# A routed two-layer kernel on one core: four input groups in flight, GpSimd's loop bounds read later, low halves ahead of VectorE's turn

## The chip, the cores and the metric

The kernel runs on 1 core of one Trainium2 chip. The metric is the device time of one execution in microseconds (us), lower is better. The kernel before was timed three times: 565.46, 571.8 and 562.29 us, median 565.46 us.

## The reference, cut to what matters

The input x is 128 graphs of 64 nodes with 128 features, 8192 tokens in all. First comes a graph attention layer over every graph, then a mixture of 8 experts of which each token takes 2:

```python
x = x + elu(softmax(where(adj > 0, leaky(e_src + e_dst), -inf)) @ (layernorm(x) @ W))   # one adjacency for all graphs
h = layernorm(x)
scores = h @ Wg.T + bg
top2, idx = top_k(scores, 2);  p = softmax(top2)
for e in range(8):                      # hidden width 512
    y = relu(h @ W1[e].T + b1[e]) @ W2[e].T + b2[e]
    out += combine[..., e] * y          # combine holds p at the two chosen experts
x = x + out
```

All data is float32.

## The kernel before, in words

The program is written engine by engine; the order on each engine is the order of the code, and engines wait for each other on semaphores only.

**Stage 1, 16 groups of 512 tokens.** Group g lies in `x_all[:, g]`. A step t works on five groups at five stages at once: normalisation and attention scores of group t, softmax and attention product of t-1, residual, second norm and gate of t-2, top-2 choice of t-3, and slot numbers of t-4. SyncE (SP) loads x in `_(sp)`: groups 0 and 1 at L399 and L405, then a loop (L408) of two bodies; body q waits for the last landing on `x_in[q]` and then issues the next group (L412), so two groups are in flight. Behind that loop stand in SP's queue the expert weights `w1_raw`, `w2_raw` (L415, L416) and biases, and then the copies of normalised rows into `rows` (L432, `pass_on`). VectorE waits for `x_in` ahead of its statistics (L812 and L1024). GpSimd waits for the last groups of x (L489, L490), then fills the sure blocks' slots with pads (L491), and from step 4 on sends each group's 1024 rows to their slots in HBM with 8 indirect DMAs (L504).

**Stage 2, expert blocks of 512 slots.** Block i is loaded into `xs`, transposed (PE L1401), rounded to a high part (ACT L681) and a low part (DVE L1107). TensorE does 12 matmuls for the hidden layer (L1417, L1418, L1421; four chunks, each with `w1_hi` on the high part, `w1_lo` on the high part, `w1_hi` on the low part), then transposes of the next block's x and of the last block's y (L1401, L1409), then 12 for the result (L1430, L1431, L1433). ScalarE (ACT) does the relus (L686, L690), the rounding of the next block and the result's bias (L696). VectorE's `turn(i, b, sent)` halves the four chunks of block i+1, makes the low part of block i+2, and weighs block i's result (`weigh`, L1122) with its row numbers (`ysi`, L1124). `ysi` releases GpSimd's `send_rows` (L521): 4 indirect DMAs per block into `moe_rows`. There are four buffers b; from block 4 on `weigh` first waits until the rows of block i-4 have landed (`scattered[b]`).

Blocks 0 to 7 (two of each of experts 0 to 3) are sure to exist; how many more each expert has is known only when all tokens are routed. `block_table()` writes `until_i` on VectorE. After its turns 1, 2 and 3 VectorE works out `pairs` and `rest`, the numbers of trips of the last loops of GpSimd and VectorE, and releases `pairs_ok`. GpSimd's `pairs_and_rest(pool)` waits for it and loads two registers from `until_i` (L368). `low_halves(e)` (L1100) makes `w1_lo` and `w2_lo` of expert e as raw minus high; it waits for ACT's `high_halves(e)` (L562, L564), and TensorE waits for it (`lo_ok`) ahead of block 2e.

The first blocks run beside the last steps of stage 1 (`drain()` on each engine). At the end SP reads the rows back (L466), TensorE, GpSimd (L529) and VectorE (L1276) add them to x, and ACT stores.

Of the kernel before, what the change touches and what calls it, by code (L numbers as in the profile page):

```python
# [21 lines left out]
GROUPS = TOKENS // GROUP  # L22
# [6 lines left out]
AHEAD = 4  # L29
# [14 lines left out]
STAGES = 5  # L44
MASKED = -1e30
META = 4
LEAD = 2
FIRST = 1
HIGH, LOW = 14, 15
# [26 lines left out]
def gnn_moe_kernel(nc, x, adj, w, wt, a, wg_t, bg, w1_t, b1_t, w2_t, b2_t, consts, out):  # L76
    ctx = ExitStack()
    with ctx:
# [3 lines left out]
        def sem(name):  # L82
            return ctx.enter_context(nc.semaphore(name))
# [40 lines left out]
        x_all = sb("x_all", [P, GROUPS, SUB, D])  # L124
# [206 lines left out]
        out_ok = sem("out_ok")  # L331
        due_met = sem("due_met")
        moe_got, moe_got1 = ([sem(f"{n}{g}") for g in range(GROUPS)] for n in ("moe_got", "moe_got1_"))
        x_in, rows_out = ([sem(f"{n}{q}") for q in range(2)] for n in ("x_in", "rows_out"))
        scattered = [sem(f"scattered{b}") for b in range(BUFS)]

        def tiles(ap):
# [27 lines left out]
        def pairs_and_rest(eng):  # L365

            eng.wait_ge(pairs_ok, 1)
            return [eng.value_load(until_i[0:1, E + n:E + n + 1], min_val=1, max_val=most) for n, most in ((0, 2 * E), (1, 2))]  # L368
# [26 lines left out]
        @block.sync  # L395
        def _(sp):
            sp.dma_start(a_sb[:, :], a).then_inc(c_a, 16)
            sp.dma_start(cst[:, :], consts).then_inc(c_cst, 16)
            sp.dma_start(x_all[:, 0, :, :], x_groups[0]).then_inc(x_in[0], 16)  # L399
            sp.dma_start(wt_sb[:, :], wt).then_inc(c_wt, 16)  # L400
            sp.wait_ge(int_zeros, 1)
            sp.dma_start(adj_i[0:NODES, 0:NODES], adj).then_inc(c_adj0, 16)
            sp.dma_start(adj_i[NODES:P, NODES:P], adj).then_inc(c_adj1, 16)
            sp.dma_start(w_sb[:, :], w).then_inc(c_w, 16)
            sp.dma_start(x_all[:, 1, :, :], x_groups[1]).then_inc(x_in[1], 16)  # L405
            sp.dma_start(wg_sb[:, :], wg_t).then_inc(c_wg, 16)
            sp.dma_start(bg_sb[:, :], bg.partition_broadcast(P)).then_inc(c_bg, 16)
            with sp.Fori(1, GROUPS // 2) as m:  # L408
                for q in range(2):

                    sp.wait_ge(x_in[q], 16 * m)
                    sp.dma_start(x_all[:, bass.ds(2 * m + q, 1), :, :],  # L412
                                 x_groups[bass.ds(2 * m + q, 1)].rearrange("g p s d -> p g s d")).then_inc(x_in[q], 16)

            sp.dma_start(w1_raw[:, :, :], w1_t).then_inc(c_w1, 16)  # L415
            sp.dma_start(w2_raw[:, :, :, :], w2_t).then_inc(c_w2, 16)  # L416
            sp.dma_start(b1_sb[:, :, :], b1_t).then_inc(c_b1, 16)
            sp.dma_start(b2_sb[:, :], b2_t).then_inc(c_b2, 16)

            def pass_on(m, q):  # L420

                g = 2 * m + q
                xn2_due, sent, passed = [v if isinstance(v, int) else nc.snap(v) for v in
                                         (SUB * g + SUB, 16 * 2 * SUB * m, 32 * g)]

                sp.wait_ge(xn2_ok, xn2_due)
                if later(m):
                    sp.wait_ge(rows_out[q], sent)
                if later(g):
                    sp.wait_ge(rowx_ok, passed)  # L430
                for k in range(2):
                    sp.dma_start(rows[q][:, k, :, 0:D], xn2[q][:, :, :]).then_inc(rowx_ok, 16)  # L432

            for q in range(2):
                pass_on(0, q)
            with sp.Fori(1, SURE_GROUPS // 2 + 1) as m:
                for q in range(2):
                    pass_on(m, q)
            pass_on(SURE_GROUPS // 2 + 1, 0)
            load_block(sp, sure_row(0), 0)  # L440
            pass_on(SURE_GROUPS // 2 + 1, 1)
            for q in range(2):
                pass_on(GROUPS // 2 - 1, q)

            sp.wait_ge(table_ok, 1)
            bounds = [SURE_BLOCKS]
            for q in range(2):
                sp.wait_ge(rows_out[q], 16 * 2 * SUB * (GROUPS // 2))
            n = sp.value_load(count_i[0:1, E - 1:E], min_val=0, max_val=TOKENS)
            for k in range(LEAD):  # L450
                sp.dma_start(slots[bass.ds(n + ((E - 1) * CAP + (k + 1) * GROUP), GROUP), :].rearrange("(p s) r -> p s r", s=SUB),
                             pad_rows[:, (E - 1) % 2, :, :]).then_inc(beyond_out, 16)
            for e in range(E - 1):
                bounds.append(block_bound(sp, e))
                sp.wait_ge(pads_out, 16 * max(e + 1, 2))
                with sp.Fori(bounds[e], bounds[e + 1]) as i:
                    row = nc.s_assert_within((i - bounds[e]) * GROUP + rest_row(e), rest_row(e), (e + 1) * CAP - GROUP,
                                             skip_runtime_bounds_check_because="an expert has at most TOKENS tokens")
                    load_block(sp, row, i)
            bounds.append(block_bound(sp, E - 1))  # L460
            sp.wait_ge(pads_out, 16 * E)
            for n in range(LEAD):
                load_block(sp, (E - 1) * CAP + n * GROUP, bounds[E - 1] + n)

            def read_plane(k, g):
                sp.dma_start(moe_in(k, g), moe_groups[k, g]).then_inc((moe_got, moe_got1)[k][g], 16)  # L466

            sp.wait_ge(late_ok, 4)
            for k in range(2):
                for h in range(GROUPS // 2):  # L470
                    due = bounds[E - 1 + k]
                    if h < GROUPS // 2 - 1:
                        due = sp.value_load(late_i[0:1, h:h + 1, k], min_val=1, max_val=MOST_BLOCKS)
                    sp.wait_ge(landed, due)
                    sp.sem_inc(due_met, 1)
                    for g in (2 * h, 2 * h + 1):
                        read_plane(k, g)

        @block.gpsimd
        def _(pool):  # L480
# [4 lines left out]
            nc.gpsimd.tensor_copy(pad_rows[:, 0, :, ID].bitcast(I32), cst[:, C_PAD:C_FULL]).then_inc(pads_ok, 1)  # L485
            nc.gpsimd.tensor_scalar(pad_rows[:, 1, :, ID].bitcast(I32), cst[:, C_PAD:C_FULL], float(GROUP), None, ALU.add).then_inc(pads_ok, 1)
            pool.wait_ge(pads_ok, 2)
            for q in range(2):
                pool.wait_ge(x_in[q], 16 * (GROUPS // 2))  # L489
            for i in range(SURE_BLOCKS):  # L490
                nc.gpsimd.dma_start(slots[sure_row(i):sure_row(i) + GROUP, :].rearrange("(p s) r -> p s r", s=SUB),  # L491
                                    pad_rows[:, i // 2 % 2, :, :]).then_inc(sure_out, 16)
# [14 lines left out]
                                in_=rows[q][:, k, j, :], in_offset=None).then_inc(rows_out[q], 16)  # L507

            by_steps(pool, step)
            pairs, rest = pairs_and_rest(pool)  # L510

            def send_rows(i, b, landings=()):

# [20 lines left out]
            for b in range(BUFS - 1):  # L534
                pool.wait_ge(scattered[b], QUADS * (16 * SUB))
            pool.sem_inc(landed, BUFS * QUADS - 1)
            with pool.Fori(0, pairs) as n:

                send_rows(2 * n + BUFS * QUADS, 0, ((3, QUADS), (1, n + QUADS)))
                send_rows(2 * n + (BUFS * QUADS + 1), 1, ((0, n + (QUADS + 1)),))  # L540
# [240 lines left out]
        def _(dve):  # L781
# [27 lines left out]
            def first_stats(b):  # L809

                for g in range(BATCHES[b].start, BATCHES[b].stop):
                    dve.wait_ge(x_in[g % 2], 16 * (g // 2 + 1))  # L812
                    for j in range(SUB):
                        last = nc.vector.bn_stats(bn1[:, g - BATCHES[b].start, j, :], x_all[:, g, j, :])
                last.then_inc(stats1_ok, 1)
                dve.wait_ge(stats1_ok, b + 1)
                for g in range(BATCHES[b].start, BATCHES[b].stop):
                    for j in range(SUB):
                        last = nc.vector.bn_aggr(mv1[:, g, j, :], bn1[:, g - BATCHES[b].start, j, :])
                last.then_inc(aggr1_ok, 1)  # L820
                dve.wait_ge(aggr1_ok, b + 1)
                nc.vector.tensor_scalar(var1[:, BATCHES[b], :], mv1[:, BATCHES[b], :, 1], EPS, None, ALU.add).then_inc(var1_ok, 1)
# [192 lines left out]
            def step(t, groups, q, m):  # L1015
# [5 lines left out]
                    add_bases(gr)  # L1021
                    write_slots(gr, q, m)
                if gx is not None and norms(gx) > 1:
                    dve.wait_ge(x_in[q], 16 * (m + 2))  # L1024
                    for j in range(SUB):
                        nc.vector.bn_stats(bn3[:, j, :], x_all[:, bass.ds(gx + AHEAD, 1), j, :].rearrange("p g d -> p (g d)"))
                if gx is not None:
# [113 lines left out]
            def turn(i, b, sent):  # L1141

                dve.wait_ge(ys_ok, i + 1 + FIRST)
                for c in range(HC):
                    halve(i + 1, c)
                low_x(i + 2)
                weigh(i, b, sent)
# [67 lines left out]
            by_steps(dve, step, GROUPS + 1)  # L1215
            drain()
            for b in range(1, BUFS):
                turn(b, b, 0)
                if b > 1:
                    low_halves(b)  # L1220
            nc.vector.tensor_scalar(until_i[:, E:E + 1], until_f[:, E - 1:E], 0.5, 0.75 - FULL, ALU.mult, ALU.add
                                    ).then_inc(blocks_ok, 1)
            dve.wait_ge(blocks_ok, 5)
# [311 lines left out]
```

## Time and profile before

| | us |
|---|---|
| three timed runs | 565.46, 571.8, 562.29 |
| median | 565.46 |
| span of the profiled execution | 568.7 |
| time of the profiled execution outside its span | not recorded |
| TensorE busy in the span | 455.3 (80%) |
| VectorE / ScalarE / GpSimd busy | 362.3 / 319.5 / 291.6 |

The span runs from the first to the last instruction of one execution. The profile was taken on one execution; a timed run may wait at other places. Start times below are counted from the span's start. In a timeline row the bracket tells how long the engine sat idle ahead of the instruction and who released it; "remote" is a releaser that the profile doesn't attribute, and "issue" is time in which the engine waited for nothing that the profile shows.

### The profile page before, as it was taken

To read this page: it belongs to the slowest core of one execution; us is meant where nothing else is said; L and a number is where in the kernel's file an instruction comes from. 1 tells how busy PE (TensorE), PEld (TensorE's weight loads), DVE (VectorE), ACT (ScalarE), POOL (GpSimd) and SP (SyncE) were. 2 spreads that over 40 slices of the span, in tenths; PEclk is the share of its full clock that TensorE was granted. 3 is DMA by queue.
4 is the path that set the end of the run, shared out by engine and by line. 5 is a ranking of instruction groups with operands and counts; after the bars stand their busy time and mean duration, and the time that the engine had idled before them with its cause. 6 is when DMAs were issued, how large, how long until landed. Compare 5 with 4: busy or idle time off the path is not lost.

```text
span 568.7 us, 9056 instructions
## 1 busy us (share of the span) xinstructions
PE 455.3 (80%) x2231; PEld 333.3 (59%) x2246; DVE 362.3 (64%) x1410; ACT 319.5 (56%) x760; POOL 291.6 (51%) x292
## 2 busy tenths in 40 slices
PE   8798377786666667868879866999999899989881
PEld 4566245564555445656658634777777687867530
DVE  6689257666556554667657625677767667756763
ACT  2778145655445455554558724667677577746600
POOL 1033755564444455445712775656765466565462
PEclk9999677878778888757989976999999999999986
DMA  5595322221122223223232312332332323256689
GB/s 137 169 378 175 93 75 72 71 80 58 42 66 70 76 76 93 65 81 94 66 108 66 85 51 73 95 99 74 93 95 72 95 74 93 79 168 203 184 270 318
DMA packets 56291, 63.03 MB, mean 111 GB/s; under 512 B 7744, under 2 KB 40896, under 8 KB 56000
## 3 DMA queue, kind: packets, MB, share of 16 engines
q1 hardware_dynamic: 35728, 33.28, 20.1%
q0 software_dynamic: 9344, 20.10, 10.5%
q10 hardware_dynamic: 11184, 9.26, 5.4%
q8 instruction: 12, 0.20, 0.1%
q14 instruction: 23, 0.19, 0.1%
HBM read 27.28 MB, written 26.94 MB: 95 GB/s over the span
## 4 chain that ended last, share of the span: by engine, by line
PE 49%; another core or an unknown queue 15%; ACT 12%; issue 9%; DVE 8%; DMA 3%; POOL 2%; SPq 1%; ACTq 0%; POOLq 0%; DVEq 0%
PE bank L1417 5%; PE bank L1421 5%; PE bank L1433 5%; PE bank L1418 4%; PE bank L1430 4%; PE bank L1431 4%; PE bank L1377 4%; PE bank L1318 4%; PE bank L1379 3%; ACT prob L591 3%; PE bank L1299 3%; PE bank L1409 2%; PE bank L1401 2%; ACT hh L690 2%
## 5 line engine op out<-in xcount | busy, mean ns | idle before, releaser
L504 POOL DMA_INDIRECT expert_slots<-rows,slot_i x128 | 127.6, 997 | 122.3 <-DVE slot_i L868 85.6
L1430 PE MATMUL bank<-hh,w_hi 128*128 128x512 f32 x144 | 63.4, 441 | 12.7 <-issue 4.5
L1417 PE MATMUL bank<-xh,w_hi 128*128 128x512 f32 x144 | 62.5, 434 | 7.3 <-ACT xh L681 4.8
L1318 PE MATMUL bank<-wh,prob_t 128*128 128x128 f32 x128 | 27.6, 383 | 48.4 <-ACT prob_t L599 39.0
L521 POOL DMA_INDIRECT moe_rows<-hrelu,ysi x40 | 41.9, 1048 | 43.1 <-issue 37.7
L696 ACT ACTIVATE yb<-bank,b_sb 128x512 f32<-128x512 f32 x36 | 24.8, 690 | 68.9 <-PE bank L1433 42.6
L1433 PE MATMUL bank<-hl,w_hi 128*128 128x512 f32 x144 | 60.6, 421 | 0.0
L1418 PE MATMUL bank<-xh,w_lo 128*128 128x512 f32 x144 | 59.5, 413 | 0.0
L1421 PE MATMUL bank<-xl,w_hi 128*128 128x512 f32 x144 | 59.2, 411 | 0.0
L1431 PE MATMUL bank<-hh,w_lo 128*128 128x512 f32 x144 | 58.5, 406 | 0.0
L521 POOL DMA_INDIRECT moe_rows<-hexp,ysi x40 | 42.6, 1065 | 26.3 <-DVE ysi L1124 13.1
L1131 DVE CAST hh<-z 128x512 fp32r<-128x512 f32 x36 | 16.5, 459 | 60.9 <-ACT z L686 52.3
L1318 PEld LDWEIGHTS bank<-wh,prob_t 128*128 128x128 f32 x128 | 23.4, 273 | 52.1 <-ACT prob_t L599 42.1
L690 ACT ACTIVATE hh<-bank,b_sb 128x512 fp32r<-128x512 f32 x72 | 50.2, 697 | 0.0
L521 POOL DMA_INDIRECT moe_rows<-xn,ysi x32 | 35.6, 1113 | 22.2 <-issue 11.8
L521 POOL DMA_INDIRECT moe_rows<-u,ysi x32 | 32.1, 1002 | 20.4 <-issue 10.3
L1430 PEld LDWEIGHTS bank<-hh,w_hi 128*128 128x128 f32 x144 | 27.8, 193 | 22.4 <-DVE hh L1131 7.2
L1417 PEld LDWEIGHTS bank<-xh,w_hi 128*128 128x128 f32 x144 | 29.0, 201 | 20.1 <-issue 9.4
L599 ACT COPY prob_t<-bank 128x512 f32<-128x512 f32 x16 | 9.4, 586 | 53.5 <-remote 49.7
L1433 PEld LDWEIGHTS bank<-hl,w_hi 128*128 128x128 f32 x144 | 27.8, 193 | 16.9 <-DVE hl L1138 7.6
L1299 PE MATMUL bank<-mask_b,ident_b 128*128 128x512 bf16 x146 | 36.4, 378 | 0.7
L686 ACT ACTIVATE z<-bank,b_sb 128x512 f32<-128x512 f32 x36 | 24.8, 688 | 15.7 <-PE bank L1421 14.2
(166 smaller groups left out, 1124.1 us busy)
## 6 DMA issues: line engine op xcount, KB each, us to landing
rows<-xn SPq DMA_DIRECT2D x32, 256.0 KB
xs<-expert_slots SPq DMA_DIRECT2D x27, 260.0 KB
x_all<-x SPq DMA_DIRECT2D x16, 256.0 KB, 2.9
w_raw<-w_t SPq DMA_DIRECT2D x2, 2048.0 KB, 12.6
w_raw<-moe_rows SPq DMA_DIRECT2D x16, 256.0 KB, 4.0
out<-x_all ACTq DMA_DIRECT2D x16, 256.0 KB
xs<-expert_slots ACTq DMA_DIRECT2D x11, 260.0 KB
w_hi<-moe_rows SPq DMA_DIRECT2D x9, 256.0 KB, 5.8
```

Source lines behind the costliest of these rows:

```text
L504: nc.gpsimd.indirect_dma_start(out=slots, out_offset=bass.IndirectOffsetOnAxis(ap=slot_i[q][:, k * SUB + j:k * SUB + j + 1], axis=0), in_= ...
L521: nc.gpsimd.indirect_dma_start(out=moe_rows, out_offset=bass.IndirectOffsetOnAxis(ap=ysi[b][:, t:t + 1], axis=0), in_=ys[b][:, t, :], in_o ...
L686: nc.scalar.activation(hr[c], ps_h[c][:, :], ACT.Relu, bias=b1_sb[:, e, c:c + 1]).then_inc(r_ok, 1)
L690: nc.scalar.activation(hh[:, c, :], ps_h[c][:, :], ACT.Relu, bias=b1_sb[:, e, c:c + 1]).then_inc(hh_odd_ok, 1)
L1299: nc.tensor.matmul(tiles(tile), ident_b[:, :], mask_b[:, :, :], start=True, stop=True)
L1318: last = nc.tensor.matmul(tiles(ps_av)[:, j, :], prob_t[:, j, :], wh[:, j, :], start=True, stop=True)
L1417: nc.tensor.matmul(ps_h[c][:, :], w1_hi[:, e, chunk], xh[:, :], start=True, stop=False)
L1418: nc.tensor.matmul(ps_h[c][:, :], w1_lo[:, e, chunk], xh[:, :], start=False, stop=False)
L1421: nc.tensor.matmul(ps_h[c][:, :], w1_hi[:, e, chunk], xl[:, :], start=False, stop=True).then_inc(h_ps, 1)
L1430: nc.tensor.matmul(ps_y[:, :], w2_hi[:, e, c, :], hh[:, c, :], start=c == 0, stop=False)
L1431: nc.tensor.matmul(ps_y[:, :], w2_lo[:, e, c, :], hh[:, c, :], start=False, stop=False)
L1433: last = nc.tensor.matmul(ps_y[:, :], w2_hi[:, e, c, :], hl[:, c, :], start=False, stop=c == HC - 1)
```

## The change

Three edits. (1) `LOADS = 4`: four semaphores `x_in`, groups 2 and 3 are issued outright, and the loop has four bodies of three trips; the waits of VectorE and GpSimd on `x_in` are renamed accordingly. (2) GpSimd's `pairs_and_rest(pool)` moves behind its loop over the first 28 blocks. (3) `low_halves(2)` and `low_halves(3)` move ahead of `turn(2)` and `turn(3)` on VectorE.

```diff
+LOADS = 4
...
+        x_in = [sem(f"x_in{n}") for n in range(LOADS)]
...
-            with sp.Fori(1, GROUPS // 2) as m:
-                for q in range(2):
-
-                    sp.wait_ge(x_in[q], 16 * m)
-                    sp.dma_start(x_all[:, bass.ds(2 * m + q, 1), :, :],
-                                 x_groups[bass.ds(2 * m + q, 1)].rearrange("g p s d -> p g s d")).then_inc(x_in[q], 16)
+            for g in range(2, LOADS):
+                sp.dma_start(x_all[:, g, :, :], x_groups[g]).then_inc(x_in[g], 16)
+            with sp.Fori(1, GROUPS // LOADS) as m:
+                for n in range(LOADS):
+
+                    sp.wait_ge(x_in[n], 16 * m)
+                    sp.dma_start(x_all[:, bass.ds(LOADS * m + n, 1), :, :],
+                                 x_groups[bass.ds(LOADS * m + n, 1)].rearrange("g p s d -> p g s d")).then_inc(x_in[n], 16)
...
-            for q in range(2):
-                pool.wait_ge(x_in[q], 16 * (GROUPS // 2))
+            for n in range(LOADS):
+                pool.wait_ge(x_in[n], 16 * (GROUPS // LOADS))
...
             by_steps(pool, step)
-            pairs, rest = pairs_and_rest(pool)
...
             pool.sem_inc(landed, BUFS * QUADS - 1)
+            pairs, rest = pairs_and_rest(pool)
             with pool.Fori(0, pairs) as n:
...
-                    dve.wait_ge(x_in[q], 16 * (m + 2))
+                    of = gx + AHEAD
+                    dve.wait_ge(x_in[of % LOADS], 16 * (of // LOADS + 1))
...
             for b in range(1, BUFS):
-                turn(b, b, 0)
                 if b > 1:
                     low_halves(b)
+                turn(b, b, 0)
```

GpSimd's queue before, from the last slot rows of stage 1 (L504) to the first rows of the loop over 28 blocks (L521):

```order
L504 DMA expert_slots<-rows,slot_i 70656x130 x128
L368 TENSOR_LOAD until_i
L368 ISA x2
L368 TENSOR_LOAD until_i
L368 ISA x2
L531 UNCONDITIONAL_BRANCH
L531 ISA
L521 DMA moe_rows<-hrelu,ysi 17408x128 x4
```

The same place now; the lines are numbered five further at most (L508 was L504, L524 was L521, L370 was L368):

```order
L508 DMA expert_slots<-rows,slot_i 70656x130 x128
L534 UNCONDITIONAL_BRANCH
L534 ISA
L524 DMA moe_rows<-hrelu,ysi 17408x128 x4
L517 REGISTER_ALU
...
L534 COMPARE_AND_BRANCH
L370 TENSOR_LOAD until_i
L370 ISA x2
L370 TENSOR_LOAD until_i
L370 ISA x2
L541 UNCONDITIONAL_BRANCH
```

Both loads and their wait went from ahead of the first block's rows to behind the 28th block's.

VectorE before, from the end of turn 1 (`hexp`, `ysi`) through turn 2 (`u`) to the start of turn 3:

```order
L1124 COPY ysi<-meta 128x4
L1131 CAST hh<-z 128x512
L1112 COPY meta<-xs 128x8
...
L1107 TENSOR_TENSOR xl<-bank,xh 128x512
L1122 TENSOR_TENSOR u<-bank,meta 128x512
L1124 COPY ysi<-meta 128x4
L1100 TENSOR_TENSOR w_lo<-w_raw,w_hi 128x512 x2
L1131 CAST hh<-z 128x512
```

The same place now:

```order
L1129 COPY ysi<-meta 128x4
L1105 TENSOR_TENSOR w_lo<-w_raw,w_hi 128x512 x2
L1136 CAST hh<-z 128x512
L1117 COPY meta<-xs 128x8
...
L1112 TENSOR_TENSOR xl<-bank,xh 128x512
L1127 TENSOR_TENSOR u<-bank,meta 128x512
L1129 COPY ysi<-meta 128x4
L1105 TENSOR_TENSOR w_lo<-w_raw,w_hi 128x512 x2
L1136 CAST hh<-z 128x512
```

The first pair of `w_lo` is expert 2's and now stands a whole turn earlier; the second is expert 3's.

## Rows read from the trace of the kernel before

**Rows 1.** The page: the span, busy time by engine, and the chain's shares.
```profile
span 568.7 us, 9056 instructions
PE 455.3 (80%) x2231; PEld 333.3 (59%) x2246; DVE 362.3 (64%) x1410; ACT 319.5 (56%) x760; POOL 291.6 (51%) x292
PE 49%; another core or an unknown queue 15%; ACT 12%; issue 9%; DVE 8%; DMA 3%; POOL 2%; SPq 1%; ACTq 0%; POOLq 0%; DVEq 0%
```

**Rows 2.** Busy time by stretch of single blocks: PE, PEld, DVE, ACT, POOL, clock, DMA.
```profile
core 0: us, PE busy (x) PEld busy (x) DVE busy (x) ACT busy (x) POOL busy (x), PEclk, DMA share, GB/s
274.50:284.30 9.80, 7.94 (x33) 5.29 (x31) 5.54 (x21) 5.23 (x9) 7.67 (x8) 0.92 0.16 53
284.30:296.40 12.10, 8.62 (x33) 5.64 (x33) 7.41 (x15) 7.27 (x13) 1.96 (x3) 0.92 0.40 127
304.50:311.00 6.50, 6.50 (x34) 5.16 (x32) 6.11 (x18) 5.90 (x10) 2.13 (x2) 1.00 0.20 55
311.00:320.20 9.20, 7.61 (x33) 4.99 (x33) 4.97 (x11) 5.89 (x10) 7.09 (x7) 1.00 0.28 75
320.20:327.10 6.90, 6.74 (x33) 5.26 (x32) 5.01 (x11) 5.89 (x10) 5.36 (x6) 1.00 0.31 86
327.10:348.10 21.00, 10.61 (x32) 6.05 (x32) 4.64 (x9) 5.18 (x8) 14.77 (x15) 0.66 0.16 50
```

**Rows 3.** VectorE's statistics from 20 to 40 us; timeline of GpSimd and SP's queue.
```profile
L1026 DVE BATCH_NORM_STATS2 bn<-x_all 128x6 f32<-128x128 f32 x4 | 0.9, 277 | 0.0
27.46 0.36 SPq L415 DMA_DIRECT2D w_raw<-w_t  x1
32.40 4.57 POOL L491 DMA_DIRECT2D expert_slots<-pad_rows  x8 [28.15 <-DMA x_all<-x]
50.94 1.04 POOL L504 DMA_INDIRECT expert_slots<-rows,slot_i  x1 [13.96 <-DVE slot_i L868]
```

**Rows 4.** Timeline of TensorE and VectorE around block 4's start.
```profile
293.89 0.39 PE L1433 MATMUL bank<-hl,w_hi 128*128 128x512 f32 x1
296.40 0.78 PE L1417 MATMUL bank<-xh,w_hi 128*128 128x512 f32 x1 [2.13 <-DVE w_lo L1100]
299.92 0.40 PE L1421 MATMUL bank<-xl,w_hi 128*128 128x512 f32 x1
290.19 0.43 DVE L1131 CAST hh<-z 128x512 fp32r<-128x512 f32 x1 [2.06 <-ACT z L686]
294.89 1.29 DVE L1100 TENSOR_TENSOR w_lo<-w_raw,w_hi 128x512 fp32r<-128x512 f32 x2
```

**Rows 5.** The chain that ended last, around 306 us: start, us, what.
```profile
306.22 0.50 POOLq L368
...
308.56 1.06 POOL moe_rows L521
312.87 2.24 DMA moe_rows<-hrelu,ysi
315.13 0.69 DVE hrelu L1122
```

**Rows 6.** Timeline of GpSimd, from the last slot rows to block 0's rows.
```profile
285.91 0.96 POOL L504 DMA_INDIRECT expert_slots<-rows,slot_i  x1 [0.30 <-issue]
308.56 1.06 POOL L521 DMA_INDIRECT moe_rows<-hrelu,ysi  x1 [21.70 <-issue]
345.17 0.96 POOL L521 DMA_INDIRECT moe_rows<-u,ysi  x1 [0.30 <-issue]
```

**Rows 7.** Timeline of ScalarE and VectorE where they wait for TensorE's signals.
```profile
287.35 0.69 DVE L1122 TENSOR_TENSOR hexp<-bank,meta 128x512 f32<-128x512 f32 x1 [2.37 <-remote]
288.82 0.69 ACT L696 ACTIVATE yb<-bank,b_sb 128x512 f32<-128x512 f32 x1 [3.51 <-remote]
335.41 0.69 ACT L686 ACTIVATE score<-bank,b_sb 128x512 f32<-128x512 f32 x1 [2.89 <-remote]
347.49 0.59 ACT L681 CAST xh<-bank 128x512 fp32r<-128x512 f32 x1 [4.45 <-remote]
```

**Rows 8.** Timeline of GpSimd at the 29th block.
```profile
494.81 0.96 POOL L521 DMA_INDIRECT moe_rows<-hrelu,ysi  x1 [1.23 <-DVE ysi L1124]
```

More of the change, by code:

```diff
@@ L333, in gnn_moe_kernel @@
         moe_got, moe_got1 = ([sem(f"{n}{g}") for g in range(GROUPS)] for n in ("moe_got", "moe_got1_"))
-        x_in, rows_out = ([sem(f"{n}{q}") for q in range(2)] for n in ("x_in", "rows_out"))
+        x_in = [sem(f"x_in{n}") for n in range(LOADS)]
+        rows_out = [sem(f"rows_out{q}") for q in range(2)]
         scattered = [sem(f"scattered{b}") for b in range(BUFS)]
@@ L811, in first_stats @@
                 for g in range(BATCHES[b].start, BATCHES[b].stop):
-                    dve.wait_ge(x_in[g % 2], 16 * (g // 2 + 1))
+                    dve.wait_ge(x_in[g % LOADS], 16 * (g // LOADS + 1))
                     for j in range(SUB):
```

## The prediction

> **What bounds the kernel now.** I read the page first. TensorE is busy for 80% of the span and makes 49% of the chain that ended last, but 15% of that chain goes to releasers that the profile can't name and 9% to "issue" [rows 1]. So TensorE is the engine to keep fed, and a quarter of the chain is waiting. Next I cut stage 2 into blocks with the busy time by stretch. A block in which nothing waits takes 6.5 us from hidden layer to hidden layer, and TensorE is busy for all of it (304.5 to 311.0) [rows 2]. Its neighbours take 9.2, 6.9 and then 21.0 us, with the same 32 or 33 matmul records each [rows 2]. These excesses are what the change can reach. The timeline tells what they are. Block 6 (311.0 to 320.2) waits for VectorE, which waits for rows of block 0 that GpSimd sent only from 308.56 on [rows 5, 6]. Block 8 (327.1 to 348.1) is different: ScalarE idles 2.89 and 4.45 us ahead of work whose TensorE input was finished long before, released by "remote" [rows 7]. All that while GpSimd issues indirect DMAs with gaps of 0.30 us, until its last at 345.17 + 0.96 = 346.1, and 1.4 us behind that ScalarE goes on [rows 6, 7]. The same stands at 277 to 288.8: waits of 2.37 and 3.51 us for "remote", beside GpSimd's last slot rows, released 1.95 us behind the last one's end (285.91 + 0.96 = 286.87) [rows 6, 7]. I call this a starved stretch: signals of TensorE arrive late while GpSimd issues without a pause. That is a reading of coincidences, not a mechanism that the trace shows.
>
> **Part 1, four groups of x in flight: 0.** SP leaves the x loop earlier, so w1, w2, the biases and the pads go out earlier. Who waits? VectorE's statistics on x_all sat idle for 0.0 us from 20 to 40 us [rows 3]. GpSimd waited 28.15 us for the last x, but its next work, the first slot rows at 50.94, then waited another 13.96 us for VectorE's slot numbers [rows 3]; that cover stays, since slot numbers don't hang on the loads. The weights, whose load was issued from 27.46 on [rows 3], are first used in step 14 of 18, far behind. No instruction is added but four waits' renaming. Bounds: nothing waited for x, so no more than the 0.0 idle can be won; more traffic beside the first steps could cost up to 1 us, as the pads' 4.57 us of issue now falls elsewhere. I take 0.
>
> **Part 2, low halves ahead of the turn: -2.1.** TensorE ends block 3 with the matmul at 293.89 and starts block 4 at 296.40, 2.13 us idle, released by w_lo [rows 4]. VectorE made that w_lo at 294.89 in 1.29 us, behind turn 2, while it had sat idle for 2.06 us ahead of turn 2's first cast at 290.19 [rows 4]. Moved there, 1.29 us fit into 2.06 us and delay nothing; its input, `high_halves(2)`, stands in ScalarE's queue ahead of the yb of 288.82 [rows 7] and is done by then. Block 4's other inputs are ready when block 3 ends, so the 2.13 us go. Behind the wait nine matmuls took from 296.40 to the next one's start at about 299.92 + 0.24, 3.8 us [rows 4]; nine of the undisturbed block's 24, with its transposes counted as four more, take 6.5 x 9 / 28 = 2.1. That could give up to another 1.4 us (I round down, as the block before was disturbed too), which I keep for the range. Expert 3's pair moves likewise and had not been waited for. At worst the pair delays turn 2 by its 1.29 us. What is late next is the starved stretch below.
>
> **Part 3, GpSimd's bounds behind 28 blocks.** Four terms.
> (a) The wait for GpSimd: block 6 took 9.2 us and block 7 6.9 where 6.5 is undisturbed [rows 2]: -2.7 - 0.4 = -3.1. With the change block 0's rows go out at about 287.2, right behind the slot rows, and have landed long before VectorE needs the buffer at 311.
> (b) GpSimd's backlog: in the profile it starts four blocks late and needs until 346.1 to catch up, and block 8 in that stretch takes 21.0 us instead of 6.5: -14.5 [rows 2, 6]. With the change it is never more than two blocks behind, and a pause stands between blocks: four DMAs take 4 x (0.96 + 0.30) = 5.0 us of a block's 6.5.
> (c) The price of starting early: at 286.87 GpSimd doesn't stop. Block 0's rows are ready, block 1's are released at about 288, so it goes on for two blocks, 10 us, to about 297. TensorE's signals, which were released at 287.35 and 288.82, would stay late for these 10 us. In block 8 a starved stretch of 21.0 us lost 14.5, that is 0.69 per us, so + 10 x 0.69 = +6.9. Bounds: 0 (from 308.56 to 326 GpSimd streamed too, and TensorE's signals were on time) and +13.8 if all four blocks follow on each other.
> (d) The loads moved to the 29th block: from 306.22 to 308.56 the two loads and what surrounds them took 2.34 us [rows 5]. At the new place GpSimd had 1.23 us of idle ahead of block 28's rows [rows 8], so 2.34 - 1.23 = +1.1 delay GpSimd, in a stretch where it is near the pace of the end. Bounds 0 and 2.3.
> The Trainium skill ("DMA: Bandwidth & Descriptors", section "Latency and other measured facts") gives a floor of about 600 ns for one such load; two would be an estimated 1.2 us and fit into the idle time, and the sum would be 1.1 us lower. The trace's 2.34 us for both is higher, and I go by it.
>
> **The sum.** 0 - 2.1 - 3.1 - 14.5 + 6.9 + 1.1 = -11.7 us. Against the profiled span: 568.7 - 11.7 = 557.0 us. The span alone is 3.2 us above the median of 565.46, and the runs spread over 9.5 us, so the profiled execution is a slow one. I take that excess as delay of this same kind, which the median execution has less of and so can't save. The predicted median is therefore 557.0 and not 553.8; the likeliest gain on the median is 8.5 us, 1.5%.
>
> **Rivals.** About 2% (11 us) is what a measurement of this kernel can tell from no change.
> 1. Block 8's stretch does not hang on GpSimd's backlog. For it: the stretch begins at 327, though GpSimd has streamed since 308.56, and block 8 is the first of the loops with loaded bounds. Against: it ends 1.4 us behind GpSimd's last DMA, as the one at 288.8 does. Then only the plain waits go: -2.1 - 3.1 + 1.1 = -4.1, from the median 561.4 us. The Trainium skill ("TensorE: Matmul & The Clock Gate", section "The cost: per-tile semaphore tail") puts an increment's cost on TensorE at about 26 ns and knows no dependence on GpSimd; by it this rival would be the likelier. The waits of 2.4 to 4.5 us behind finished matmuls [rows 7] don't agree with it, so I keep the rival below one half.
> 2. The early start costs nothing: (c) is 0, as from 308.56 to 326. Then 568.7 - 2.1 - 1.4 - 3.1 - 14.5 + 1.1 = 548.7 us.
> 3. Slower. The starved stretch feeds itself: late signals make VectorE's weighing late, blocks 1 to 3 reach GpSimd bunched, and it streams without a pause for four blocks, 20 us, +13.8; and a stretch like block 8's still comes later, so that (b) is not won. - 2.1 - 3.1 + 13.8 + 1.1 = +9.7, from the median 575.2 us. It decides if GpSimd's DMAs of blocks 0 to 3 follow each other with 0.30 us gaps until past 305.
> 4. The edits do nothing measurable: part 1's earlier traffic shifts the steps of stage 1, in which similar late signals stand, at random. That is the scatter of a few us around each case.
>
> **Chances.** Forecast 0.46, rival 1 0.22, rival 2 0.18, rival 3 0.14. Range: down to rival 2's 548 and up past rival 1's 561 and half-way to rival 3, 569; so 548 to 569. Below 554.2 (2%) lies nearly all of rival 2 and a quarter of the forecast's case with a little of rival 1: 0.30. Above 576.8 lies less than half of rival 3: 0.05. The rest, 0.65, is within 2%.
>
> **What would show it.** In the profile of the changed kernel: SP's w1 load issued some us ahead of 27.46, and the first slot rows still waiting for slot_i near 51 (part 1 right). No wait of TensorE on w_lo at block 4 (part 2). GpSimd's first L521-group DMA about 0.3 us behind the last slot rows and no VectorE wait for landed rows in turns 4 to 6 (3a). Block 8 at 6.5 to 8 us (3b). "Remote" waits of ScalarE reaching on to about 297 and blocks 2 to 3 together some 7 us longer than their 9.8 + 12.1 [rows 2], less part 2's 2.1 (3c). GpSimd's pause of about 2.3 us before the 29th block (3d). I am wrong if a stretch of late signals as long as block 8's stands elsewhere in stage 2, if stage 1 moves by more than a few us, or if VectorE or ScalarE now waits for the pads or weights.

## The result and the profile after

The changed kernel takes 544.93 us (median of 541.87, 542.93, 546.94 and 547.95) beside 567.86 us for the kernel before on the same chip (562.29 to 571.8). The ratio is 0.9656, 95% interval 0.959 to 0.9721: 3.4% faster. Ratios here compare fast runs alone, so they differ somewhat from the quotient of two medians. The forecast was 557.0 us in a range of 548 to 569, so the time lies 3.1 us below the range's low end, and nearest to rival 2. The profiled execution's span fell from 568.7 to 546.0 us, by 22.7, where the sum said 11.7.

The page of the changed kernel: span, busy time, chain. To be held against [rows 1].

```profile
span 546.0 us, 9056 instructions
PE 443.0 (81%) x2246; PEld 330.6 (61%) x2246; DVE 362.3 (66%) x1410; ACT 318.7 (58%) x760; POOL 288.2 (53%) x292
PE 57%; another core or an unknown queue 13%; ACT 11%; issue 8%; DVE 6%; DMA 2%; SPq 2%; ACTq 1%; DVEq 0%; POOL 0%; POOLq 0%
```

TensorE makes 57% of the chain, not 49; the releasers without a name still make 13%. GpSimd is gone from it.

Where [rows 3] had SP's w1 load, GpSimd's pads and its first slot rows, the timeline of the changed kernel has:

```profile
18.82 0.36 SPq L419 DMA_DIRECT2D w_raw<-w_t  x1
23.73 4.55 POOL L495 DMA_DIRECT2D expert_slots<-pad_rows  x8 [19.76 <-DMA x_all<-x]
42.58 1.55 POOL L508 DMA_INDIRECT expert_slots<-rows,slot_i  x1 [14.30 <-DVE slot_i L872]
```

The load and the pads stand 8.6 and 8.7 us earlier. So do, by 8.4 us, the first slot rows, though both profiles name `slot_i` as their releaser. Of the next three rows the first is from the kernel before, the second from the changed kernel's second profile (e5), the third from the bounds' move alone, with two groups in flight (e7):

```profile
40.20 0.22 DVE L868 TENSOR_REDUCE slot_i<-slot_p 128x8 int32<-128x64 f32 x1
43.66 1.04 POOL L508 DMA_INDIRECT expert_slots<-rows,slot_i  x1 [15.49 <-DMA rows<-xn]
50.29 1.04 POOL L504 DMA_INDIRECT expert_slots<-rows,slot_i  x1 [15.23 <-DMA rows<-xn]
```

The slot numbers of group 0 were there at 40.20 in the kernel before, 10.7 us ahead of the first slot rows at 50.94. So something else held GpSimd: by e5's and e7's rows the copy of the normalised rows into `rows`, which SP issues behind the weights. In all four profiles with two groups of x in flight the first slot rows stand at 49.3 to 50.9, in all ten with four at 42.0 to 43.7.

GpSimd's timeline from its last slot rows on (to be held against [rows 6]; every DMA between two rows shown follows with 0.3 us of idle):

```profile
276.08 0.96 POOL L508 DMA_INDIRECT expert_slots<-rows,slot_i  x1 [1.66 <-issue]
...
285.98 1.44 POOL L508 DMA_INDIRECT expert_slots<-rows,slot_i  x1 [0.30 <-issue]
287.72 0.96 POOL L524 DMA_INDIRECT moe_rows<-hrelu,ysi  x1 [0.30 <-issue]
...
307.57 0.96 POOL L524 DMA_INDIRECT moe_rows<-xn,ysi  x1 [0.30 <-issue]
316.43 0.96 POOL L524 DMA_INDIRECT moe_rows<-hrelu,ysi  x1 [7.89 <-DVE ysi L1129]
```

Block 0's rows now go out behind the last slot rows (287.72, before 308.56). But GpSimd then streams on for all four first blocks, until 308.53, 32.5 us without a break since 276.08. ScalarE's waits of that time, where [rows 7] had its own:

```profile
275.75 0.69 ACT L700 ACTIVATE yb<-bank,b_sb 128x512 f32<-128x512 f32 x1 [4.80 <-remote]
295.62 0.69 ACT L690 ACTIVATE prob_t<-bank,b_sb 128x512 f32<-128x512 f32 x1 [2.18 <-remote]
307.76 0.69 ACT L700 ACTIVATE yb<-bank,b_sb 128x512 f32<-128x512 f32 x1 [9.37 <-remote]
```

Busy time by stretch, same columns as [rows 2]: an undisturbed stretch from the transposes of block 4's x on; the stretch with the long wait; the two blocks behind it, each from its first matmul for the result (L1435) to the next block's; the first 2.9 us of these apart; and one later stretch.

```profile
284.05:292.90 8.85, 8.85 (x47) 7.13 (x45) 6.87 (x14) 6.11 (x12) 6.78 (x7) 1.00 0.49 161
299.30:311.10 11.80, 4.77 (x20) 3.43 (x18) 1.66 (x12) 1.86 (x3) 7.10 (x8) 0.79 0.18 59
311.10:319.19 8.09, 8.09 (x33) 6.52 (x33) 6.21 (x14) 7.39 (x14) 2.15 (x3) 0.78 0.16 43
319.19:325.65 6.46, 6.46 (x36) 5.33 (x34) 4.95 (x12) 5.90 (x11) 4.31 (x5) 1.00 0.28 82
311.10:314.00 2.90, 2.90 (x7) 2.28 (x8) 2.72 (x6) 2.90 (x7) 0.00 (x0) 0.50 0.35 92
327.10:333.60 6.50, 6.47 (x32) 5.06 (x31) 4.57 (x11) 5.64 (x11) 4.34 (x5) 1.00 0.26 78
```

So the long stretch of block 8 (327.1 to 348.1 before) is gone; in its place stands one at 299 to 311, and it costs twice. TensorE stood idle for most of it, and in the first 2.9 us behind it the granted clock is 0.50, the 1.2 GHz level. The first block behind it takes 8.1 us with TensorE busy all the time, the second 6.5, which is what an undisturbed one takes. So the wait's second price is 1.6 us.

A cut of the whole program is more use than any single wait. The table is worked out from TensorE's timeline of each kernel: the start of the transposes of block 3's x, from there to block 10's, and from there to the end of the span.

| one profile each | up to block 3 | blocks 3 to 10 | rest | span |
|---|---|---|---|---|
| before | 277.3 | 75.0 | 216.4 | 568.7 |
| before, second profile (e6) | 282.6 | 73.3 | 210.2 | 566.1 |
| changed | 275.3 | 62.8 | 207.9 | 546.0 |
| changed, second profile (e5) | 269.6 | 64.8 | 209.1 | 543.5 |
| e1, without the bounds' move | 275.7 | 78.6 | 208.1 | 562.4 |
| e7, the bounds' move alone | 275.0 | 63.1 | 208.3 | 546.4 |
| e2, without the x loads | 277.9 | 58.0 | 207.9 | 543.8 |
| e3, without the low halves | 270.9 | 64.4 | 209.1 | 544.4 |
| e8, pauses between first blocks | 269.5 | 66.8 | 208.2 | 544.5 |
| e4, pause in stage 1 | 263.1 | 58.4 | 209.1 | 530.6 |
| e9, other work in stage 1 | 249.6 | 68.5 | 206.5 | 524.6 |
| e10, pauses in stage 2 | 278.0 | 52.0 | 221.7 | 551.7 |
| e11, both pauses | 245.8 | 56.6 | 226.8 | 529.2 |
| e12, two pauses in stage 1, and e10's | 239.7 | 56.9 | 229.6 | 526.2 |

Seven undisturbed blocks would take 45.5 us, so the middle column holds what the late signals cost there.

### The profile page after: what moved, and what is told of

It reads as the page before. It is cut to its first block, busy times and chain, and to the rows that moved or that the text cites. A ratio compares the mean times of both kernels' runs of the same rounds, so it can differ in the third digit from the quotient of the medians.

```text
span 546.0 us, 9056 instructions
## 1 busy us (share of the span) xinstructions
PE 443.0 (81%) x2246; PEld 330.6 (61%) x2246; DVE 362.3 (66%) x1410; ACT 318.7 (58%) x760; POOL 288.2 (53%) x292
## 4 chain that ended last, share of the span: by engine, by line
PE 57%; another core or an unknown queue 13%; ACT 11%; issue 8%; DVE 6%; DMA 2%; SPq 2%; ACTq 1%; DVEq 0%; POOL 0%; POOLq 0%
PE bank L1438 6%; PE bank L1422 6%; PE bank L1435 6%; PE bank L1426 5%; PE bank L1436 5%; PE bank L1423 5%; PE bank L1323 5%; PE bank L1382 4%; ACT prob L595 4%; PE bank L1384 3%; PE bank L1304 2%; PE bank L1414 2%; PE bank L1406 2%; ACT xn L635 1%
## 5 line engine op out<-in xcount | busy, mean ns | idle before, releaser
L508 POOL DMA_INDIRECT expert_slots<-rows,slot_i x128 | 126.7, 990 | 132.4 <-DVE slot_i L872 94.7
L1323 PE MATMUL bank<-wh,prob_t 128*128 128x128 f32 x128 | 29.2, 400 | 51.4 <-ACT prob_t L603 45.1
L1435 PE MATMUL bank<-hh,w_hi 128*128 128x512 f32 x144 | 62.2, 432 | 5.7 <-DVE hh L1136 3.1
L1422 PE MATMUL bank<-xh,w_hi 128*128 128x512 f32 x144 | 60.6, 421 | 0.8 <-ACT xh L685 0.8
L1436 PE MATMUL bank<-hh,w_lo 128*128 128x512 f32 x144 | 58.4, 406 | 0.0
L1323 PEld LDWEIGHTS bank<-wh,prob_t 128*128 128x128 f32 x128 | 25.0, 291 | 55.0 <-ACT prob_t L603 47.9
L524 POOL DMA_INDIRECT moe_rows<-hrelu,ysi x40 | 41.4, 1035 | 30.5 <-issue 15.1
L524 POOL DMA_INDIRECT moe_rows<-hexp,ysi x40 | 41.8, 1045 | 22.8 <-issue 13.1
L524 POOL DMA_INDIRECT moe_rows<-u,ysi x32 | 32.5, 1017 | 21.2 <-issue 11.0
L524 POOL DMA_INDIRECT moe_rows<-xn,ysi x32 | 34.5, 1077 | 16.8 <-issue 11.5
L1304 PE MATMUL bank<-mask_b,ident_b 128*128 128x512 bf16 x160 | 39.4, 378 | 0.0
L1435 PEld LDWEIGHTS bank<-hh,w_hi 128*128 128x128 f32 x144 | 27.7, 193 | 12.7 <-DVE hh L1136 5.1
L1426 PEld LDWEIGHTS bank<-xl,w_hi 128*128 128x128 f32 x144 | 28.2, 196 | 7.0 <-DVE xl L1112 0.2
```

What stands on the lines that cost most here:

```text
L508: nc.gpsimd.indirect_dma_start(out=slots, out_offset=bass.IndirectOffsetOnAxis(ap=slot_i[q][:, k * SUB + j:k * SUB + j + 1], axis=0), in_= ...
L524: nc.gpsimd.indirect_dma_start(out=moe_rows, out_offset=bass.IndirectOffsetOnAxis(ap=ysi[b][:, t:t + 1], axis=0), in_=ys[b][:, t, :], in_o ...
L1304: nc.tensor.matmul(tiles(tile), ident_b[:, :], mask_b[:, :, :], start=True, stop=True)
L1323: last = nc.tensor.matmul(tiles(ps_av)[:, j, :], prob_t[:, j, :], wh[:, j, :], start=True, stop=True)
L1422: nc.tensor.matmul(ps_h[c][:, :], w1_hi[:, e, chunk], xh[:, :], start=True, stop=False)
L1426: nc.tensor.matmul(ps_h[c][:, :], w1_hi[:, e, chunk], xl[:, :], start=False, stop=True).then_inc(h_ps, 1)
```

## The experiments

The theory: TensorE's completion signals reach ScalarE and VectorE late while GpSimd issues indirect DMAs without a break; the bounds' move takes GpSimd's backlog away, and with it one stretch. The rivals: the stretch has another cause, or another edit brought the gain.

**e1, the bounds' loads back ahead of the loop.**

```diff
             by_steps(pool, step)
+            pairs, rest = pairs_and_rest(pool)
...
-            pairs, rest = pairs_and_rest(pool)
```

> The change with GpSimd's bounds read ahead of the first block again; x loads and low halves as changed. Theory (most of the gain is the bounds' move): the wait of VectorE for landed rows at turn 4 (4 us) and a block of some 20 us around block 8 are back, and the time is 10 to 18 us above the changed kernel's 545, so 555 to 563 us. Rival (the late starved stretch is chance, the gain lies in the x loads or elsewhere): 545 to 550 us.

Measured 564.1 us, ratio 0.9873 [0.9799, 0.9948], the kernel before at 571.36. GpSimd and ScalarE in its timeline:

```profile
305.60 1.28 POOL L525 DMA_INDIRECT moe_rows<-hrelu,ysi  x1 [20.29 <-issue]
...
341.88 0.96 POOL L525 DMA_INDIRECT moe_rows<-u,ysi  x1 [0.30 <-issue]
345.69 0.69 ACT L700 ACTIVATE yb<-bank,b_sb 128x512 f32<-128x512 f32 x1 [13.85 <-remote]
```

GpSimd stands for 20.29 us, then streams until 342.8, and the long wait is back in that stream. This edit carries most of the gain.

**e2, the x loads back to two in flight** (edit 1 of the change undone, all else as changed).

> The change with two groups of x in flight as before; bounds and low halves as changed. Theory (x loads are worth nothing, as the sum put them): 543 to 548 us, stage 1 as long as in the changed kernel. Rival (stage 1 is 2 us shorter and the later blocks steadier because of the earlier loads): 550 us or more.

Measured 553.33 us, 0.9725 [0.9649, 0.9801]. The intervals of this and the changed kernel overlap, and the profiled execution, at 545.6, was its fastest. Up to block 3 it is 277.9 beside 275.3 and 269.6. By its median the time came as the rival had it (550 or more), and it is not alone: of the kernels with the bounds' move, the two with two groups in flight have medians of 553.33 and 552.8 us (e2, e7), and three with four groups 544.93, 546.99 and 545.43 (changed, e5, e3). The profiles show a path for it. With two groups the slot rows of group 0 go out so late that those of group 1 follow at once, in one stream of 16 DMAs (50.94 to 71.48 in the kernel before); the changed kernel has two streams of eight there, 3.5 us apart. The slot numbers of group 2 then stand at 74.8 to 77.0 us in the four profiles with two groups in flight, and at 71.9 at the latest in the ten with four. So the x loads are likely worth some us. But the intervals overlap, and e7's runs alone reach from 540.32 to 558.6, so how many is open.

**e3, the low halves back behind their turns** (edit 3 undone).

> The change with low halves behind the turn as before. Theory (worth 2.1 us, in one place): TensorE waits about 2 us on w_lo at block 4 again and the time is 545 + 2 = 547 us. Rival (it hides behind the starved stretch, which now lies in the same blocks): 545 us.

Measured 545.43 us, 0.9479 [0.9373, 0.9585]: no loss, as the rival had it. TensorE doesn't wait on `w_lo` at block 4 in its profile, and the middle is 64.4 us, the same as with the edit.

**e4, a pause in stage 1.** The changed kernel, and GpSimd waits until all its slot rows so far have landed before the second half of each group.

```diff
                     for k in range(2):
+                        if k:
+                            pool.wait_ge(rows_out[q], 16 * (2 * SUB * (gr // 2) + SUB))
                         for j in range(SUB):
```

> The changed kernel, but GpSimd waits between the fourth and the fifth of a group's eight slot DMAs until the first four have landed, so that it never issues for 10 us without a pause. Theory (signals of TensorE are held up by GpSimd's unbroken issuing): the waits of 3 to 5 us of ScalarE for the turned probabilities, 53 us over 12 steps, shrink to below 2 us each, and the time falls by 15 to 35 us, to 510 to 530 us. Rival (they are held up by something else and end by chance with the stream): the waits stay and the time is 545 us or some us more for the longer GpSimd step.

Measured 533.58 us, 0.9358 [0.9287, 0.9428]. A wait was added to the engine in question, and the program is about 11 us faster than the changed kernel, though less than the 15 to 35 us expected. ScalarE's groups for the attention product's input, over all 16 groups, in the changed kernel, in e4 and in e9 below (busy, mean ns | idle before and its releasers):

```profile
L603 ACT COPY prob_t<-bank 128x512 f32<-128x512 f32 x16 | 9.4, 585 | 56.1 <-remote 53.0 <-PE bank L1313 3.1
```

```profile
L605 ACT COPY prob_t<-bank 128x512 f32<-128x512 f32 x16 | 9.4, 586 | 24.7 <-PE bank L1315 19.3 <-remote 5.4
```

```profile
L609 ACT COPY prob_t<-bank 128x512 f32<-128x512 f32 x16 | 9.4, 586 | 19.7 <-PE bank L1319 10.0 <-issue 9.7
```

On this tile the 53.0 us of "remote" fall to 5.4 and to none. Over all tiles less is gone. Up to the first transposes of stage 2 the remote waits of ScalarE add to 56.3 us in the changed kernel, 49.2 in e4 and 30.0 in e9, those of VectorE to 32.1, 5.5 and none. In e4 most of ScalarE's late signals only moved to other tiles (`xn_t` 20.5, `z` 13.2 us), and VectorE was relieved.

**e5 and e6, the changed kernel and the one before once more; e7, the bounds' move alone.**

> The changed kernel once more, as a reference beside the next ones. Both theories: 542 to 548 us. For its trace: if the starved stretches hang on GpSimd's unbroken issuing, there is one of them at blocks 3 to 6 again and none from block 10 to the end; if they are chance, they stand elsewhere.

> The kernel before once more, for a second profile. Theory (a stretch hangs on GpSimd's backlog of four blocks): block 6 waits for landed rows and one block from 6 to 9 takes 15 to 22 us, as in the first profile; from block 10 to the last transposes it takes 175 us where the first profile had 184, if that excess was chance. Rival (chance): no such block, or it stands elsewhere.

> The kernel before with the bounds' move alone. Theory (the move makes nearly all of the gain): 548 to 556 us, 15 to 20 us below the kernel before. Rival (the sum as predicted, -9.6 us for this edit): 558 to 562 us.

e5: 546.99 us beside 569.39 for the kernel before, which scattered from 554.31 to 579.0 there, so the ratio is 0.9836 [0.9701, 0.9971]. e6: 567.91 us in one execution. e7: 552.8 us (540.32 to 558.6). The long wait in e6's, then in e5's timeline, each behind GpSimd's last DMA; in e6 with TensorE's last matmul ahead of it for the result that `yb` reads:

```profile
326.67 0.50 PE L1433 MATMUL bank<-hl,w_hi 128*128 128x512 f32 x1
342.10 0.96 POOL L521 DMA_INDIRECT moe_rows<-u,ysi  x1 [0.30 <-issue]
346.41 0.69 ACT L696 ACTIVATE yb<-bank,b_sb 128x512 f32<-128x512 f32 x1 [18.03 <-remote]
```

```profile
295.47 0.96 POOL L524 DMA_INDIRECT moe_rows<-u,ysi  x1 [0.30 <-issue]
298.30 0.69 ACT L700 ACTIVATE yb<-bank,b_sb 128x512 f32<-128x512 f32 x1 [13.92 <-remote]
```

So the stretch at blocks 8 and 9 belongs to the kernel before, and the shorter one at blocks 3 to 6 to the changed one. In e6 ScalarE waited 18.03 us in one piece, for a matmul that had ended 19.2 us before. What did not come again are the late waits of the first profile (216.4 us for the rest, against 206.5 to 210.2 in ten others): those were chance.

**e8, a pause between the first blocks.** GpSimd waits for its landed rows ahead of block 0 and behind each of blocks 0 to 3.

```diff
+            for q in range(2):
+                pool.wait_ge(rows_out[q], 16 * 2 * SUB * (GROUPS // 2))
+            for b in range(BUFS):
+                send_rows(b, b)
+                pool.wait_ge(scattered[b], 16 * SUB)
-            with pool.Fori(0, QUADS) as m:
+            with pool.Fori(1, QUADS) as m:
```

> The changed kernel, but GpSimd lets each of the first four blocks' rows land (and stage 1's slot rows ahead of them) before it goes on, so that its 32 us of unbroken issuing from 276 to 308 is cut by pauses of 2 us. Theory (the unbroken issuing holds TensorE's signals up): the 9.4 us wait of ScalarE at 298 is gone, blocks 3 to 6 take 7 us each and the time falls by 8 to 14 us, to 531 to 537. Rival (not the issuing): a block of 15 us or more stays and the time is 545 or a few us more.

Measured 547.93 us (538.37 to 549.6): the rival's number, not the theory's. GpSimd and ScalarE:

```profile
295.42 1.21 POOL L524 DMA_INDIRECT moe_rows<-u,ysi  x1 [2.08 <-DMA moe_rows<-hexp,ysi]
302.62 1.18 POOL L524 DMA_INDIRECT moe_rows<-xn,ysi  x1 [2.08 <-DMA moe_rows<-u,ysi]
309.90 1.04 POOL L524 DMA_INDIRECT moe_rows<-hrelu,ysi  x1 [2.23 <-DMA moe_rows<-xn,ysi]
333.34 1.24 POOL L524 DMA_INDIRECT moe_rows<-xn,ysi  x1 [8.37 <-DVE ysi L1134]
```

```profile
304.99 0.69 ACT L705 ACTIVATE yb<-bank,b_sb 128x512 f32<-128x512 f32 x1 [0.55 <-PE bank L1443]
311.45 0.69 ACT L705 ACTIVATE yb<-bank,b_sb 128x512 f32<-128x512 f32 x1 [0.55 <-PE bank L1443]
325.57 0.69 ACT L705 ACTIVATE yb<-bank,b_sb 128x512 f32<-128x512 f32 x1 [8.21 <-remote]
```

While the pauses last, `yb` waits 0.55 us. They also cost GpSimd 2.1 us per block, so its backlog stays; from 309.90 it works that off without a break until 325.0, and there stands the long wait. The stretch had only moved.

**e9, other work in the place of e4's wait.**

```diff
                     for k in range(2):
+                        if k:
+                            for n in (1, 2):
+                                nc.gpsimd.memset(fill[:, :], 0.0).then_inc(fill_ok, 1)
+                                pool.wait_ge(fill_ok, 2 * gr + n)
                         for j in range(SUB):
```

> As e4, but in the place of the wait for landed rows GpSimd fills a scratch buffer twice (0.97 us each in the trace, some 2.2 us with the two gaps) between the 4th and 5th slot DMA of every group. The question is what about the pause helped. Theory 1, it is the break in the issue of indirect DMAs: any other work there does the same, time 531 to 538 us, the first transposes of stage 2 near 232, few waits of ScalarE on prob_t. Theory 2, it is GpSimd standing idle, or its DMAs having landed, that lets TensorE's signals through: 541 to 550 us, first transposes near 245, prob_t waits as in the changed kernel (53 us in 12).

Measured 528.04 us, 0.92 [0.9126, 0.9274], the kernel before at 573.95. As theory 1 asks, GpSimd need not stand idle: two memsets for nothing, 2.00 us a group, do at least as well as the wait. Whether its DMAs must have landed is not settled, though. The memsets and their gap make a break of 2.28 us, and the waits for landed rows in e4 are 1.6 to 3.6 us, so in e9 too the rows may often have landed by then. Stage 2 has no such break, and one block there, in busy time by stretch, reads:

```profile
277.70:306.00 28.30, 12.31 (x38) 8.10 (x39) 7.96 (x18) 9.85 (x17) 16.46 (x17) 0.58 0.15 49
```

This is the longest of all, 28.3 us at a clock of 0.58, with a stream of GpSimd from 264.23 to 295.2 in it.

**e10, a pause behind every second block; e11, that and e4's; e12, that and two pauses per group in stage 1.**

```diff
                 for b in range(BUFS):
                     send_rows(BUFS * m + b, b)
+                    if b % 2:
+                        pool.wait_ge(scattered[b], (m + 1) * (16 * SUB))
```

> The changed kernel, but in the loop over 28 blocks GpSimd waits behind every second block until that block's rows have landed (some 2.1 us, so 6.1 us per block against TensorE's 6.5). It never streams for more than two blocks, 10 us. Theory (late signals come with an unbroken stream): no stretch of late signals in stage 2 longer than 2 to 3 us a time, blocks 3 to 12 together below 70 us (undisturbed 65), time 533 to 538 us. Rival (the stretch is only moved, as in e8, or comes with the backlog itself): some block still takes 13 to 20 us, time 543 to 550.

> e4's pause in stage 1 and e10's in stage 2. If both theories hold and the places are independent, the gains add: e4's 533.6 less the some 10 us that its block of 16.6 us lost, so 521 to 527 us. If e10 gains nothing in itself, 531 to 537.

> As e11, but in stage 1 each group's 8 slot DMAs are broken in two places, behind the 3rd and the 6th, each time until all have landed. Theory (a stream of some 6 us already brings late signals; e4 still shows waits of 2.5 to 4.2 us): those waits shrink, 3 to 8 us below e11. Rival (the extra pauses make GpSimd late with the last slot rows, which stage 2's first block loads wait for): 1 to 5 us above e11.

e10: 556.46 us (542.21 to 569.07), 0.9767 [0.9698, 0.9836]; e11: 537.92, 0.9398 [0.9337, 0.946]; e12: 527.84, 0.9136 [0.904, 0.9231]. For e10 and e11 neither side's number came; e12 lies 10 us below e11, a little more than expected. In e10 blocks 3 to 10 take 52.0 us, the least of all kernels, though one wait of 6.71 us is left there (300.96), behind 16 DMAs in one stream; and the rest takes 221.7 instead of some 208, in e11 226.8 and in e12 229.6. The pause stands between pairs of blocks, so eight DMAs follow each other, 10 us, where the changed kernel issues four at a time with breaks of 1.2 to 2.9 us; and in such pairs ScalarE waits for `yb` again (3.61 us in e10 at 335.90, 5.24 us in e11 at 351.24). Behind the 28 blocks, where the pauses end, comes a longer one. e11, in the loop behind them:

```profile
458.98 0.95 POOL L526 DMA_INDIRECT moe_rows<-hrelu,ysi  x1 [1.88 <-issue]
460.23 0.96 POOL L526 DMA_INDIRECT moe_rows<-hrelu,ysi  x1 [0.30 <-issue]
...
471.77 0.96 POOL L526 DMA_INDIRECT moe_rows<-hrelu,ysi  x1 [0.30 <-issue]
474.65 0.69 ACT L704 ACTIVATE yb<-bank,b_sb 128x512 f32<-128x512 f32 x1 [10.77 <-remote]
```

A backlog is worked off there in one stream of 13.7 us, as in e8. From 340 us on ScalarE's remote waits add to 19 to 22 us in e10 to e12, and to 3.6 to 5.0 in the eight other profiles with the bounds' move. That the pairs and this backlog account for all of the 14 to 22 us is my reading; no run tests it by itself. For e11 the gains did not add: its ratio is no better than e4's 0.9358. e12's second pause in stage 1 does pay, as the intervals of e12 and e11 lie apart; up to block 3 it takes 239.7 us, e11 245.8. e12 without its pauses in stage 2 was not run. e9 to e12 ran on another chip than e1 to e8, so only their ratios compare with the others.

## Why the prediction was right or wrong

**Part 1 (0).** The w1 load and the pads came earlier, as forecast. The step that failed is "that cover stays, since slot numbers don't hang on the loads": the first slot rows waited not for the slot numbers but for the rows' copy behind the weights, and came 8.4 us earlier, where the sign said near 51. The term of 0 had no reason left. What it is worth is open; e2 and e7 point to some us.

**Part 2 (-2.1).** The wait was real: e6 and e7, which lack this edit, have 1.47 and 2.18 us of TensorE on `w_lo`, and the changed kernel has none. Its worth was not: e3, which lacks the edit too, has no such wait and loses nothing (middle 64.4, with it 62.8 and 64.8). My reading is that TensorE waits for something else in these blocks anyway. The step that failed is "the 2.13 us go"; I had named what is late next and still counted the term in full.

**Part 3 (a) and (b), -3.1 and -14.5.** Right, place and mechanism: e1 brings the stretch back, e7 removes it by the bounds' move alone. Rival 1 is out.

**(c), +6.9.** Right in kind. A new stretch stands behind the last slot rows; rival 2, which came nearest in time, is not what happened. I had GpSimd stop after two blocks at about 297. In the profile it went on for four, as rival 3's sign said, but not for rival 3's reason. The `ysi` of blocks 1 to 3:

```profile
281.74 0.22 DVE L1129 COPY ysi<-meta 128x4 int32<-128x4 int32 x1
287.69 0.22 DVE L1129 COPY ysi<-meta 128x4 int32<-128x4 int32 x1
299.19 0.16 DVE L1129 COPY ysi<-meta 128x4 int32<-128x4 int32 x1
```

The kernel before had blocks 1 and 2 at 287.96 and 294.82. So they came earlier, not late: two blocks were ready when GpSimd's last slot rows ended at 287.4, the third half a microsecond later, and block 3 before GpSimd reached it at 303.79. In e5, where VectorE's weighing of block 2 did wait 5.82 us for "remote", GpSimd sent three blocks and then stopped. Rival 3's other half, a later stretch as well, did not come.

**(a) to (c) together.** In the middle column the kernels with the bounds' move take 62.8, 64.8, 63.1, 58.0 and 64.4 us (mean 62.6), those without 75.0, 73.3 and 78.6 (mean 75.6): 13.0 us. My terms for this place, part 2's among them, add to 12.8. The agreement is better than the terms deserve: part 2 is nothing, and three neighbouring stretches of one kind had been given separate prices.

**(d), +1.1.** Wrong, it is 0. The place that answers to [rows 8] in the changed kernel:

```profile
476.58 1.00 POOL L524 DMA_INDIRECT moe_rows<-hrelu,ysi  x1 [1.25 <-DVE ysi L1129]
```

The idle time ahead of the 29th block is 1.25 us, before 1.23. The two loads are not even in it. GpSimd's own queue ran them beside the DMAs of the 28th block, which it issued from 469.85 to 475.34 (min, median and max in ns, then first and last start):

```profile
L370 POOLq TENSOR_LOAD <-until_i x2: 308/402/497, 471.4 to 472.2; - x2
```

The 2.34 us of [rows 5] had held more than the two loads, and I had wrongly added them to the engine's time. The Trainium skill's floor of about 600 ns for such a load ("DMA: Bandwidth & Descriptors", section "Latency and other measured facts") led nearer to the result than my term, but the trace doesn't agree with it: the two took 0.31 and 0.50 us.

**From the span to the median.** "The profiled execution is a slow one. I take that excess as delay of this same kind, which the median execution has less of and so can't save." The kernel before later had medians of 567.9, 571.4, 569.4 and 574.0 us; the profile was an ordinary execution, and the three shown runs were quicker than most that followed. The excess had also nothing to do with blocks 3 to 10 (75.0 and 73.3 us in the two profiles). Without this step the forecast would have been 553.8 on the shown median and 556.2 on the one measured (567.86 - 11.7), and rival 2, the range's low end, 545.5; so even then 544.93 lay just outside. The measured gain is 22.9 us, and the 11.2 that the sum lacks are outside the part that I had priced. In the first two profiles 2.0 us lie ahead of block 3 and 8.5 in the rest, where the first profile of before had waits that did not come again. With both profiles of each kernel it is 7.5 ahead of block 3 (280.0 against 272.5) and 4.8 in the rest (213.3 against 208.5). Two profiles of one kernel differ by up to 6 us in either place, and e4 and e11, which run the same instructions up to block 3 but ran on two chips, by 17.3 us there. The x loads are the edit with a path into stage 1; how much of the 7.5 us it makes stays open.

## What to carry to other kernels

A wait that ends on "remote" though its producer is long done is worth an experiment, not a footnote: put a break into whatever another engine issues all that time. Two memsets in the middle of each run of eight indirect DMAs took the ratio to the kernel before from 0.9656 to 0.92, more than the whole change had brought. But a pause only helps where the engine has time for it. Where it makes a backlog (e8, e10), the backlog is worked off in one stream, and late signals come back there. Where an instruction waits for several signals, the releaser that the profile names can be the wrong one: ask when it was done. `slot_i` was there 10.7 us before the DMA that was said to wait for it. And a profile's distance from a median of three is no reason to discount a gain.

## What the runs showed of the hardware

ScalarE waited up to 18.03 us for a signal of TensorE whose matmul had ended before (e6) while GpSimd issued indirect DMAs of 0.96 us with gaps of 0.30 us, and the longest waits mostly ended 0.6 to 3.4 us behind the last of them (in the changed kernel during the last one; in e8 one of 8.73 us ended at 273.44, with more of the stream to come). A break with 2.00 us of memset in each group of eight brought the remote waits of ScalarE and VectorE in stage 1 from 88.4 us down to 30.0. Not every stream makes a long wait: in e4 GpSimd streamed from 269.49 to 296.8 and the longest wait in it was 3.97 us. The Trainium skill ("TensorE: Matmul & The Clock Gate", section "The cost: per-tile semaphore tail") has some 26 ns for an increment and nothing of another engine; the waits here are far longer. What the two share, a port, a queue or the memory of descriptors, no run here tells. The second price is the clock: behind the long waits of the changed kernel, e5 and e6 TensorE starts again at 0.50, the 1.2 GHz level, for the next 2.9 us, and in the changed kernel the first block took 8.1 instead of 6.5 us, its mean clock 0.78.
